# The order of a convolution tower's steps: one written list over four rounds, with the end of each round placed among the next round's first-layer steps

## What is computed

```python
CONVS = [(128, 10, 5)] + [(128, 3, 2)] * 4 + [(128, 2, 2)] * 2      # channels, taps, stride
for w, g, b, s in zip(conv_ws, ln_gs, ln_bs, strides):
    h = conv1d(h, w, s)
    h = fp32_layernorm(h over channels, g, b)
    h = gelu(h, approximate=False)
```

## Time and profile before

| | |
|---|---|
| median of three runs | 936.58 us |
| the profiled execution, and its span | 938.41 us, 936.5 us |
| mean granted TensorE clock over the span | 0.939 |
| busy: TensorE, VectorE, ScalarE, GpSimd | 782.9, 601.4, 307.4, 216.9 us |
| tower: first matmul of layer 0, first `half` of layer 1 | 56.99 us, 65.73 us |
| tower: start of rounds 1, 2 and 3 (their first `half`) | 174.84, 282.47, 393.12 us |
| first matmul after the tower | 556.08 us |

### The profile page before, as it was taken

How to read it: one execution, slowest core, us unless ns; L and a number is a source line. 1 busy time by engine, 2 the same in 40 slices (tenths; PEclk the granted TensorE clock), 3 DMA queues, 4 the chain that set the end, 5 groups by cost and what they waited for, 6 DMA issues and landing times. The chain is left out here.

```text
span 936.5 us, 12160 instructions
## 1 busy us (share of the span) xinstructions
PE 782.9 (84%) x4371; PEld 585.4 (63%) x4371; DVE 601.4 (64%) x1445; ACT 307.4 (33%) x506; POOL 216.9 (23%) x253
## 2 busy tenths in 40 slices
PE   0059999899979999799989767878788888799987
PEld 0016655466645655466656456877788887689977
DVE  4917746685557846414555556799889989654377
ACT  0033424433542325434232220502232331146433
POOL 3100000000000000000000002646678879148301
PEclk9999998899988999799999759999999999999999
DMA  1350340005100060000000016000000000200000
GB/s 57 44 128 1 45 99 1 1 4 108 33 1 1 13 119 0 0 1 1 1 1 1 0 49 264 1 1 1 1 1 1 1 1 1 73 4 1 1 1 26
DMA packets 22564, 25.45 MB, mean 27 GB/s; under 512 B 17052, under 2 KB 21212, under 8 KB 21404
## 3 DMA queue, kind: packets, MB, share of 16 engines
q1 hardware_dynamic: 22508, 24.74, 11.2%
HBM read 21.05 MB, written 3.66 MB: 26 GB/s over the span
## 5 line engine op out<-in xcount | busy, mean ns | idle before, releaser
L564 PE MATMUL ps<-h,w 128*128 128x400 f32 x720 | 293.9, 553 | 1.4 <-ACT h L632 1.3
L564 PEld LDWEIGHTS ps<-h,w 128*128 128x128 f32 x720 | 141.4, 203 | 107.1 <-issue 104.5
L724 DVE COPY h<-ps 128x800 f32<-128x800 f32 (+2 forms) x58 | 56.6, 976 | 100.3 <-PE ps L564 99.6
L577 PEld LDWEIGHTS ps<-averager,sq 128*100 128x100 f32 (+2 forms) x1024 | 100.0, 172 | 23.3 <-ACT sq L625 19.0
L625 ACT ACTIVATE sq<-h 128x800 f32<-128x800 f32 (+2 forms) x58 | 49.8, 859 | 180.8 <-DVE h L724 180.8
L577 PE MATMUL ps<-averager,sq 128*100 128x1 f32 (+2 forms) x1024 | 100.5, 228 | 8.8 <-ACT sq L625 8.4
L632 ACT ACTIVATE h<-h,lnp 128x800 f32<-128x800 f32 (+2 forms) x58 | 60.5, 1043 | 83.4 <-DVE h L755 81.5
L1075 PE MATMUL pt<-for_pe,ident 128*128 128x156 f32 (+2 forms) x420 | 68.2, 322 | 23.5 <-DVE for_pe L1274 23.5
L755 DVE TENSOR_TENSOR h<-h,ps 128x400 f32<-128x400 f32 (+2 forms) x116 | 60.0, 559 | 38.8 <-PE ps L593 38.8
L604 ACT ACTIVATE h<-ps,lnp 128x800 f32<-128x800 f32 x64 | 63.4, 1011 | 64.7 <-PE ps L525 64.5
L1112 POOL MEMSET eye<- 128x169 f32 x1 | 0.2, 242 | 362.6 <-PE pt L860 362.6
(11 more groups left out here) (272 smaller groups left out, 1154.6 us busy)
## 6 DMA issues: line engine op xcount, KB each, us to landing
late<-windows_dram SPq DMA_DIRECT2D x24, 375.0 KB, 7.6
gate_w<-in_gate_w SPq DMA_DIRECT2D x1, 3456.0 KB, 12.8
up_w<-in_up_w SPq DMA_DIRECT2D x1, 3456.0 KB, 19.1
windows_dram<-parts SPq DMA_DIRECT2D x12, 250.0 KB, 6.2
acts<-in_down_w SPq DMA_DIRECT2D x1, 1728.0 KB, 9.7
w<-in_w SPq DMA_DIRECT2D x1, 1024.0 KB, 6.1
xs<-in_x SPq DMA_DIRECT2D x4, 252.5 KB, 4.6
out_tokens<-hidden SPq DMA_DIRECT2D x6, 96.0 KB, 1.6
```

What stands on the lines that cost most here:

```text
L564: mm = pe.matmul(out, w[:, L.first_tap + t, :], source(l, s, 2 * p + c, t), start=(t == 0), stop=(t == L.taps - 1))
L577: mm = pe.matmul(var_ps[0:L.w, at:at + 1], sq[:, n["var"] % 2, c, q * L.w:(q + 1) * L.w], averager[:, 0:1], start=True, stop=True)
L724: nc.vector.tensor_copy(joined(l, s, p, r).rearrange("p (c b) t -> p c b t", c=2), ypair[n["bank"]][:, :, 0:L.cols].rearrange("p c (b t) - ...
```

## The change

The loop over rounds is gone: `tower_plan` writes out one list of steps for the whole tower, and `Origin`, `for_rounds` and `AHEAD` go. `ROUND_ORDER` is one turn. A step with `+` belongs to the next round, one with `-` to the round before; turns -1 to 4 are written out one after the other, and steps of rounds that do not exist are dropped. `LAST_ORDER` is layers 4 to 6, after all turns.

What is then where: seven `first` stand ahead of the first `half` of a round, where nine stood. The end of layer 3 (`scale.3.0`, `var.3.1.0`, `norm.3.1.0`, `rows.3.1.0`, `scale.3.0.1`, `scale.3.1`) stands among the layer-1 and layer-2 steps of the next round. The `first` of the next round and the scales are in another order. The first three parts of `prep` of a round stand in the turn before its usual place. Layer 4 begins after the last scale of layer 3.

With that come more buffers: four sets of `rparts` and `rows` in place of two (`SETS`), and columns of their own in the `var` bank for each layer and slot. There are also some more waits: each `var` waits for the first operation of the newest `norm` ahead of it, `rows` waits for the copy of the `rows` before, and `norm` waits for the transposes of four sets before. The wait values are now constants. The matmuls and all other arithmetic are the same in kind and number.

```diff
-AHEAD = GROUP + 1
...
+SETS = 4
...
+ROUND_ORDER = """
+    prep.0.0.3 conv.1.0.0 -scale.3.0.0 half.1.0.1 -var.3.1.0 first.0.1.1 prep.0.0.4 conv.1.0.1 var.1.0.0 first.0.0.6 prep.0.0.5
+    -norm.3.1.0 half.1.0.2 prep.0.0.6 first.0.0.7 var.1.0.1 conv.1.0.2 prep.0.0.7 prep.0.0.8 half.1.0.3 prep.0.0.9 first.0.1.3
+    conv.1.0.3 half.1.1.0 first.0.1.5 var.1.0.2 first.0.1.7 prep.0.0.10 var.1.0.3 norm.1.0.0 first.0.1.6 conv.1.1.0 half.1.1.1
+    rows.1.0.0 first.0.1.4 prep.0.0.11 prep.0.0.12 conv.1.1.1 half.1.1.2 var.1.1.0 scale.1.0.1 scale.1.0.2 conv.1.1.2 scale.1.0.6
+    scale.1.0.0 gelu.1.0.0 half.1.1.3 prep.0.0.13 var.1.1.1 scale.1.0.3 gelu.1.0.1 scale.1.0.5 -rows.3.1.0 conv.1.1.3 scale.1.0.7
+    gelu.1.0.3 +phases.0.0.0 half.2.0.0 var.1.1.2 +prep.0.0.0 scale.1.0.4 gelu.1.0.2 var.1.1.3 norm.1.1.0 conv.2.0.0 half.2.0.1
+    -scale.3.0.1 -gelu.3.0.0 rows.1.1.0 conv.2.0.1 scale.1.1.0 scale.1.1.1 gelu.1.1.0 var.2.0.0 +first.0.0.2 scale.1.1.5 scale.1.1.4
+    gelu.1.1.2 var.2.0.1 scale.1.1.3 scale.1.1.2 gelu.1.1.1 norm.2.0.0 +first.0.0.5 half.2.1.0 scale.1.1.6 scale.1.1.7 gelu.1.1.3
+    conv.2.1.0 rows.2.0.0 half.2.1.1 +prep.0.0.1 conv.2.1.1 +first.0.0.4 scale.2.0.1 scale.2.0.0 gelu.2.0.0 var.2.1.0 +first.0.0.3
+    scale.2.0.2 scale.2.0.3 gelu.2.0.1 var.2.1.1 -scale.3.1.0 -scale.3.1.1 -gelu.3.1.0 norm.2.1.0 half.3.0.0 conv.3.0.0 rows.2.1.0
+    +first.0.0.0 scale.2.1.1 scale.2.1.0 gelu.2.1.0 +first.0.1.2 var.3.0.0 scale.2.1.2 scale.2.1.3 gelu.2.1.1 half.3.1.0
+    +first.0.0.1 norm.3.0.0 conv.3.1.0 +half.1.0.0 +first.0.1.0 +prep.0.0.2 rows.3.0.0
+"""
+
+LAST_ORDER = """
+    half.4.0.0 conv.4.0.0 half.4.0.1 var.4.0.0 conv.4.0.1 half.4.1.0 var.4.0.1 norm.4.0.0 conv.4.1.0 half.4.1.1 rows.4.0.0
+    scale.4.0.0 scale.4.0.1 gelu.4.0.0 var.4.1.0 conv.4.1.1 scale.4.0.2 scale.4.0.3 gelu.4.0.1 half.5.0.0 var.4.1.1 norm.4.1.0
+    conv.5.0.0 rows.4.1.0 scale.4.1.0 scale.4.1.1 gelu.4.1.0 var.5.0.0 scale.4.1.2 scale.4.1.3 gelu.4.1.1 norm.5.0.0 half.5.1.0
+    rows.5.0.0 scale.5.0.0 scale.5.0.1 gelu.5.0.0 conv.5.1.0 half.6.0.0 var.5.1.0 norm.5.1.0 conv.6.0.0 rows.5.1.0 scale.5.1.0
+    scale.5.1.1 gelu.5.1.0 var.6.0.0 norm.6.0.0 half.6.1.0 rows.6.0.0 scale.6.0.0 scale.6.0.1 gelu.6.0.0 conv.6.1.0 var.6.1.0
+    norm.6.1.0 rows.6.1.0 scale.6.1.0 scale.6.1.1 gelu.6.1.0
+"""
+
+
+def steps_of(order):
+
+    for word in order.split():
+        what, l, s, p = word.lstrip("+-").split(".")
+        yield what, {"+": 1, "-": -1}.get(word[0], 0), int(l), int(s), int(p)
+
+
+def tower_plan():
...
+    for turn in range(-1, ROUNDS + 1):
+        for what, later, l, s, p in steps_of(ROUND_ORDER):
+            r = turn + later
+            if what in ("prep", "phases"):
+                if 0 <= r < ROUNDS - 1:
+                    order.append((what, r + 1, l, s, p))
+            elif 0 <= r < ROUNDS:
+                order.append((what, r, l, s, p))
+    for what, _, l, s, p in steps_of(LAST_ORDER):
+        order.append((what, ROUNDS - 1, l, s, p))
     return counted(order)
...
+        set_of = {(r, l, s): n["norm"] % SETS for what, r, l, s, p, n in plan if what == "norm"}
+        conv_at = [(r, l, s, p) for what, r, l, s, p, n in plan if what == "conv"]
+        square_of = {at: k for k, at in enumerate(conv_at)}
+        var_from = {1: 0, 2: 64, 3: 96, 4: 112, 5: 144, 6: 160}
+        var_at = lambda l, s, k: var_from[l] + 4 * LAYERS[l].chunks * s + k
...
+                for r in range(1, ROUNDS):
+                    scratch = windows(r, r < ROUNDS - 1)
+
+                    for slot in range(2):
+                        sp.wait_ge(y_ready, max(batch_taken(r - 1, GROUP * slot + b) for b in range(GROUP)))
+                        back(scratch, slot)
...
+                for what, r, l, s, p, n in plan:
+                    L = LAYERS.get(l)
+                    if what in ("half", "first") and n["before"]:
+                        user, number = n["before"]
+                        if user == "first":
+                            pe.wait_ge(y_taken, number + 1)
+                        else:
+                            pe.wait_ge(y_copied, number + 1)
+                    if what == "first":
+                        pe.wait_ge(win_in[s], SLOT_IN * (r + 1))
+                        first(s * GROUP + p, n["bank"])
+                    elif what in ("half", "conv"):
+                        c = int(what == "conv")
+                        if what == "half" and n["conv"] == 0:
+                            pe.wait_ge(weights_ready, 2)
+                        if l == 1:
+                            pe.wait_ge(y_taken, batch_taken(r, GROUP * s + 2 * p + c))
+                        elif l == 4:
+                            newest = r if (s, p) == (1, 1) else r - 1
+                            pe.wait_ge(gelu_done, gelus_before(plan, newest, 3, 1)[0] + 1)
+                        else:
+                            done = gelus_before(plan, r, l - 1, s)
+                            pe.wait_ge(gelu_done, done[min(2 * p + c, max(done))] + 1)
...
+                    elif what == "var":
+                        pe.wait_ge(y_taken, number_of(plan, "conv", r, l, s, p, "pair") + 1)
+                        if n["norm"]:
+                            pe.wait_ge(var_read, n["norm"])
...
+                    elif what == "rows":
+                        pe.wait_ge(rstd_ready, number_of(plan, "norm", r, l, s, 0, "norm") + 1)
+                        if n["rows"]:
+                            pe.wait_ge(rows_ready, n["rows"])
...
+                    elif what == "scale":
+                        pe.wait_ge(rows_ready, number_of(plan, "rows", r, l, s, 0, "rows") + 1)
+                        if n["scale"] >= 2:
+                            pe.wait_ge(scaled, n["scale"] - 1)
+                        pe.matmul(spread[n["scale"] % 2][:, 0:L.cols], pick[:, p, :],
+                                  rows[:, set_of[r, l, s], 0:L.cols], start=True, stop=True).then_inc(bc_ready, 1)
...
+                for what, r, l, s, p, n in plan:
+                    L = LAYERS.get(l)
+                    if what == "first":
+                        first(s, p, n["bank"], n["pair"])
+                    elif what == "conv":
+                        act.wait_ge(y_copied, n["conv"] + 1)
+                        if n["conv"] >= 2:
+                            act.wait_ge(var_done, number_of(plan, "var", *conv_at[n["conv"] - 2], "var") + 1)
+                        act.activation(sq[:, square_of[r, l, s, p] % 2, :, 0:L.cols].rearrange("p c (b t) -> p c b t", t=L.pos),
+                                       joined(l, s, p, r).rearrange("p (c b) t -> p c b t", c=2), ACT.Square).then_inc(y_taken, 1)
+                    elif what == "gelu":
+                        act.wait_ge(scaled, n["scale"])
+                        both = joined(l, s, p, r)
+                        act.activation(both, both, ACT.Gelu, scale=lnp[:, 2 * l:2 * l + 1],
+                                       bias=lnp[:, 2 * l + 1:2 * l + 2]).then_inc(gelu_done, 1)
...
+                    elif what == "norm":
+                        k, a, wide = 4 * L.chunks, set_of[r, l, s], L.w
...
+                        if n["norm"] >= SETS:
+                            dve.wait_ge(rstd_turned, n["norm"] - SETS + 1)
```

More of the change, by code:

```diff
@@ L117, in newton_rsqrt @@
     steps.settle()
-def round_plan(last):
-    order = []
[L128 to L229, removed]
@@ L230, in round_plan @@
     return counted(order)
 def counted(order):
-    n = dict.fromkeys(("pair", "half", "conv", "var", "norm", "rows", "scale", "gelu", "first", "prep"), 0)
+    n = dict.fromkeys(("pair", "half", "conv", "var", "norm", "rows", "scale", "gelu", "first", "prep", "phases"), 0)
     out, bank, held = [], 0, None
-    users = [("first", -2), ("first", -1)]
-    for what, l, s, p in order:
+    users = [None, None]
+    for what, r, l, s, p in order:
         step = dict(n)
@@ L252, in counted, with number_of, gelus_before @@
             step["bank"], held = held, None
-        out.append((what, l, s, p, step))
+        out.append((what, r, l, s, p, step))
         n[what] += 1
         n["pair"] += what in ("conv", "first")
[L256 to L276, removed]
+    return out
+def number_of(plan, what, r, layer, slot, p, kind):
+    return next(n[kind] for *key, n in plan if key == [what, r, layer, slot, p])
+def gelus_before(plan, r, layer, slot):
+    return {p: n["gelu"] for what, of, l, s, p, n in plan if (what, of, l, s) == ("gelu", r, layer, slot)}
 def conv_tower(nc, io, res, top):
-    body, per = round_plan(False)
-    last, _ = round_plan(True)
+    plan = tower_plan()
     sem = lambda n: top.enter_context(nc.semaphore(n))
@@ L457, in _ @@
                 attention_weights(sp, io, res)
-                read = number_of(body, "first", 0, 1, GROUP - 1, "pair") + 1
-                def middle(r, more):
-                    scratch = windows(r, more)
-                    sp.wait_ge(y_ready, AHEAD + per["pair"] * (r - 1))
-                    back(scratch, 0)
```

(18 more changed lines are left out.)

211 lines of the change are left out of this document (58 added, 153 removed).

## The result

The changed kernel takes 907.12 us (median of four runs, 904.04 to 910.49) where the kernel before takes 936.21; the ratio is 0.9695, 95% interval 0.9648 to 0.9742. The forecast was 914, with a range of 890 to 932 and a chance of 0.77 for faster by over 1%. The profiled execution took 910.49 us, with a span of 908.8 for 936.5 before.

The account below looks back on a forecast made before the run. TensorE's list of steps was taken to bound the kernel, losing time to idling and a falling clock. Terms -1.5 - 27.1 + 7.6 - 2.0 = -23.0 us gave 915.4 profiled, about 914 beside the median; range 890 to 932.

Parts of the forecast that it names:

- The mechanism: TensorE's list of steps sets the pace; the new order covers most chains, cutting idle time from 8.3 us a round to 3.5.
- The start: Ahead of the first `half`, seven `first` instead of nine: 2 us less, 0.5 given back for slot 1's windows, -1.5 us.
- The rounds: Rounds 0 to 2: 90.0 us of work, 3.5 idle and 6.6 clock make 100.1 each; -27.1 us for three.
- The term of 1.0 for the windows: At `+first.0.0.2`, the first to need the new windows: TensorE idle 1.0 us because their read-back lands at 60.4.
- The clock: In each round, four falls of TensorE's clock at 1.65 us, 6.6 us, behind stretches without a pair.
- The last round: No next round or layer 4 beside it: 87.6 us work, 8.6 idle, 6.6 clock make 102.8, +7.6 us.
- Layers 4 to 6: After all rounds: old order, less one `var`, `rows` and two scales counted in the last round's sum, -2.0 us.
- the rest I cost at nothing: Whole tower: removing the loop's register arithmetic and branch, one more round written out, and the new waits change nothing.
- Full clock: TensorE's clock falls nowhere in the rounds, saving 26.4 us more: 887 us, chance 0.17.
- Long falls: In layers 2 and 3 the clock stays low between pairless stretches, 17 us a round: 955 us, chance 0.10.
- The windows came in time: Against this, a rival had the read-back 4 us later, holding `+first.0.0.2` in three rounds: +17, 931 us, chance 0.10.
- TensorE did not stay idle: Against this, a rival had VectorE hand results late, TensorE idle 8.3 us a round: +19, 933 us, chance 0.10.

Follow-up runs that it names:

- the late windows: Changed kernel with the read-back of slot 0's windows held until `conv.2.0.1` of the round before was issued: 932.45 us, ratio 0.9912.
- the later set: Changed kernel unaltered, run again side by side with three edits of its last round and `var` placing: 907.36 us, ratio 0.9672.

## Why the prediction was right, and which terms were off

**The mechanism** was right: in the changed order TensorE's list runs with almost no idle time, and putting the end of layer 3 back costs 25 us. Against the old order in the same form, the tower has 25.5 us of idle time for 39.1, and 437.5 busy for 443.5. The size is off by 5 of 28 us in the spans: the rounds gained 10.5 more than forecast, and the last round, layers 4 to 6 and the rest of the kernel lost 2.9, 1.7 and 1.7 more.

**The start**: -1.5 forecast, -2.1 measured.

**The rounds**: 100.1 each forecast, 96.6 in the mean. Idle time was 3.5 forecast and 0.95 found in round 1. Only the wait for the copy of `rows`, 1.3 plus 0.2 in the walk, is there, at 0.8. The term of 1.0 for the windows was not idle time at all, although the room is 1 us at most, as the late windows showed. I walked the round at full clock and added the falls afterwards; but a fall ahead of a wait makes TensorE come later, and the wait can be gone by then. No run shows that by itself. The clock was 6.6 forecast, and 95.4 - 90.0 = 5.4 measured.

**The last round**: +7.6 forecast, +10.5 measured. My 87.6 us of work left out the end of layer 3 of round 2, 2.3 us, which I had counted in round 0 where it is not; in the whole sum that cancels. The bare norm is there at 3.09 for 3.3, but the idle time of the whole round is 105.7 - 99.2 = 6.5 us where I walked 8.6; the 0.6 for the GELU, for one, did not come. The clock cost 99.2 - 89.9 = 9.3 where I took 6.6. The experiment with layer 4 among it gives back 13 us, with one wait of 0.35.

**Layers 4 to 6**: -2.0 forecast, -0.3 measured. The work went, and most of it came back as clock: 0.75 where it was 0.80.

**The written-out form** is the step that failed: "the rest I cost at nothing", and it is worth 7 of some 30 us. I compared round 0 (written out) with round 1 (in the loop), named the slow start of round 0 but did not take it off, and left out that the loop's second pass, round 2, was 3 us longer than its first. The sum did not suffer, since I walked the new rounds from nothing and did not subtract single gains from the old ones; what suffered is the account of where the gain comes from: 7 us from the form and 24 from the order by the later set (0.9672 / 0.9927 = 0.974), 22 by the first comparison (0.9695). The row of 2.53 us at the head of the second pass is an engine that stands though it waits for nothing that the profile shows; the first pass, begun at 175.72 us, has no such wait. The Trainium skill ("Runtime: NRT & Kernel Launch", Instruction fetch mechanics) has a taken branch break the sequential prefetch of instructions, and the engine stand until the target is fetched when it is not among the pages already loaded. The row agrees with it, but that it makes up the 7 us was not shown.

**The signs.** The rounds are 96 to 97 us apart, and single pairs are slow, as forecast. The waits of 3 to 4 us a round are not there, nor is one at a `first`. "About 9 us" of idle time between `conv.3.1.0` and `half.4.0.0` was my sum for the whole last round; its terms for that place make 6.4, and the waits there are 1.17 + 0.29 + 3.09 = 4.6.

**The rivals.** Full clock did not come: 0.95 in the rounds. Long falls did not come either. The windows came in time, and TensorE did not stay idle. That the falls come where the stretch without a pair is longest, as I took it, does not hold: in round 1 of the changed kernel 4.5 us of scales, `var` and `first` (224.73 to 229.23) are followed by a half pair at full clock, and the 2.9 us of the fall shown above were not:

```profile
224.73 0.50 PE L497 MATMUL ps<-rows,pick 96*128 96x400 bf16 x2
225.07 1.49 PE L481 MATMUL ps<-averager,sq 128*100 128x1 f32 x16
...
227.19 1.50 PE L481 MATMUL ps<-averager,sq 128*100 128x1 f32 x16
228.56 0.50 PE L497 MATMUL ps<-rows,pick 96*128 96x400 bf16 x2
...
229.23 2.28 PE L469 MATMUL ps<-h,w 128*128 128x400 f32 x6
```

In the second trace of the changed kernel the clock falls within the same stretch of round 0 (4.21 us for the half pair behind it). What sets the place of a fall stays open. The two traces of the changed kernel have two or three in each of rounds 1 and 2, and the one with the two `var` apart has two.

## What to carry to other kernels

Where engines walk one list in order, price an order as a whole, by walking all engines through it: a part moved alone can land behind something that the rest of the new order had cleared away. When steps are moved to cover a stretch, look at once at the last iteration, which has nothing of a next one beside it; here filling it was worth another 13 us. And short waits on TensorE are to be priced with the clock that may fall behind them: with `prep` early, 3.3 us more of idle time came with 13.3 us more of busy time. But that price is not in proportion: with the end of layer 3 in its own turn, 13.4 us more of idle time came with 0.7 us more of busy time in the trace.
